# Scan layers of a four-layer network: the coefficients made inside the recurrence's phase, and another end for the last block

## What is computed

```python
xr, gate = split(x @ W_in.T, 2)                     # 1024 columns each
xc = silu(causal_conv4(xr + t_emb) + b_conv)
xn = layernorm(xc) * ln_g + ln_b
Bm, Cm, dt = split(xn @ W_xproj.T, 3)               # 16 states each
dt = tanh(dt @ W_dt.T + b_dt) * 0.01
Ad = 1.0 - dt * tanh(A_log)
Bd = Bm * minimum(norm(xn), 1.0)
h = clip(h * ad[:, :, None] + bd[:, :, None] * xt[:, None, :], -10.0, 10.0)   # 128 steps
yt = einsum('bd,bdh->bh', ct, h)
out = (ys + D * xn) * silu(gate) @ W_out.T
```

## Time and profile before

| | us |
|---|---|
| median of 3 runs | 4326.25 (4320.41, 4326.63, 4326.25) |
| the profiled execution | 4321.35, span 4319.3 |
| TensorE, matmuls, busy | 3880.4 (90%) |
| VectorE busy | 2926.8 (68%) |
| GpSimd busy | 1807.9 (42%) |
| ScalarE busy | 1318.1 (31%) |
| DMA, mean | 144 GB/s, 620 MB |
| granted TensorE clock, mean | 0.938 |

### The profile page before, as it was taken

The page is one execution under the profiler, slowest core; times in us unless marked ns, Lnnn a source line. Parts: engine busy times, 40 slices in busy tenths (PEclk is TensorE's granted clock), DMA queues, the critical chain, the costliest instruction groups (busy, mean ns, idle before and its releaser), DMA issues. The chain is left out here.

```text
span 4319.3 us, 67813 instructions
## 1 busy us (share of the span) xinstructions
PE 3880.4 (90%) x24096; PEld 2388.2 (55%) x24096; DVE 2926.8 (68%) x3026; ACT 1318.1 (31%) x1957; POOL 1807.9 (42%) x1456
## 2 busy tenths in 40 slices
PE   8999729999997899999889999997999819999999
PEld 6776403334333677777666777765777503343334
DVE  4666458999995666666456656643666548999996
ACT  3554301111111433333243333323554401111111
POOL 2555425555554133332312333332455425555554
PEclk9999858999999899999979999998999958999999
DMA  3665545556553222221221222223566555655663
GB/s 114 227 227 218 214 148 181 183 186 193 176 182 122 80 63 78 75 74 62 76 97 57 75 74 74 67 69 124 189 228 229 209 170 171 193 175 183 188 192 105
DMA packets 270819, 620.34 MB, mean 144 GB/s; under 512 B 34144, under 2 KB 37216, under 8 KB 270592
## 3 DMA queue, kind: packets, MB, share of 16 engines
q1 hardware_dynamic: 270592, 617.26, 43.1%
HBM read 380.71 MB, written 236.45 MB: 143 GB/s over the span
## 5 line engine op out<-in xcount | busy, mean ns | idle before, releaser
L1123 DVE CUSTOM_DVE_ANT_0 l0r_g<-l0r_g,l0r_pv,l0r_cf 128x1024 f32<-128x1024 f32 x512 | 674.3, 1339 | 76.5 <-PE l0r_pv L985 52.1
L1123 DVE CUSTOM_DVE_ANT_0 l3r_g<-l3r_g,l3r_pv,l3r_cf 128x1024 f32<-128x1024 f32 x512 | 674.1, 1339 | 75.5 <-PE l3r_pv L985 51.8
L985 PE MATMUL l0r_pv<-l0r_x,l0r_wv 32*128 32x512 f32 x1024 | 261.4, 510 | 26.3 <-POOL l0r_wv L910 20.8
L985 PE MATMUL l3r_pv<-l3r_x,l3r_wv 32*128 32x512 f32 x1024 | 260.6, 509 | 25.6 <-POOL l3r_wv L910 20.1
L997 PE MATMUL l0r_py<-l0r_g,l0r_cd 128*32 128x512 f32 x2048 | 282.0, 623 | 1.3 <-POOL l0r_cd L923 1.3
L997 PE MATMUL l3r_py<-l3r_g,l3r_cd 128*32 128x512 f32 x2048 | 281.1, 622 | 1.0 <-POOL l3r_cd L923 1.0
L985 PEld LDWEIGHTS l0r_pv<-l0r_x,l0r_wv 32*128 32x128 f32 x1024 | 97.2, 187 | 327.9 <-issue 224.8
L985 PEld LDWEIGHTS l3r_pv<-l3r_x,l3r_wv 32*128 32x128 f32 x1024 | 96.9, 186 | 326.3 <-issue 223.5
L1779 DVE RECIPROCAL l1h_rec<-l1h_ps_o 128x256 f32<-128x256 f32 x64 | 112.3, 1754 | 121.8 <-PE l1h_ps_o L1480 121.7
L1779 DVE RECIPROCAL l2h_rec<-l2h_ps_o 128x256 f32<-128x256 f32 x64 | 112.3, 1754 | 120.4 <-PE l2h_ps_o L1480 120.4
L1858 POOL TENSOR_TENSOR l2h_st<-l2h_veps,l2h_mhalf 128x1 f32<-128x1 f32 x32 | 17.6, 548 | 391.7 <-DVE l2h_veps L1745 391.7
(11 more groups left out here) (427 smaller groups left out, 9871.2 us busy)
## 6 DMA issues: line engine op xcount, KB each, us to landing
xhl_s<-l0a_xo SPq DMA_DIRECT2D x128, 512.0 KB, 4.6
l0r_x<-xhl_s SPq DMA_DIRECT2D x128, 512.0 KB, 11.7
xhl_s<-l3a_xo SPq DMA_DIRECT2D x128, 512.0 KB, 4.6
l3r_x<-xhl_s SPq DMA_DIRECT2D x128, 512.0 KB, 11.7
gate_s<-l0a_gate SPq DMA_DIRECT2D x64, 256.0 KB, 3.4
dx_s<-l0a_dx SPq DMA_DIRECT2D x32, 512.0 KB, 5.1
l0r_crow<-feed_s SPq DMA_DIRECT2D x64, 256.0 KB
l0r_dx<-dx_s SPq DMA_DIRECT2D x32, 512.0 KB, 13.3
```

The lines of the kernel that those rows point to most:

```text
L985: last = pe.matmul(pv[j % 2][:, h * HALF:(h + 1) * HALF], wv[r, q, 2 * t + j % 2, :], x[r, q, t, j % 2, :], start=True, stop=True)
L1123: dve._custom_dve(bass.dve_ops.TENSOR_ADD_SAT, out=g[:, t, j, :], in0=g[:, (t - 1) % TS, j, :], in1=pv[j % 2][:, :], s0=cf[:, q, t, 0, j:j ...
```

## The change

The coefficient phase goes; its body stands at the start of each engine's program in the recurrence's phase. Its large tiles become parts of `g`, `zh`, `zl` and `pv`, which the recurrence doesn't need yet. SP loads the constants, then x of blocks 0 and 1, dx and gate of block 0, and only then waits for `feed`, stores it and loads `crow` of both blocks. VectorE's chain has three of its steps in another place: the copies before the norm; the readers' factor before the bounds; the negative bound behind the feed's low half. GpSimd waits for `const` and the chain's 19th step before `bounds(0)`.

At the end TensorE turns block 30's second half, does the four half read-outs of block 31, then block 30's mix with block 31's first turn after its fourth slot, the second turn, and block 31's mix. VectorE, which has nothing to do after the last clamp-add, adds dx and multiplies by gate straight from `py`, in two halves of 512 columns; ScalarE makes `zh` straight from `pz` (without `zt`), VectorE `zl` from `pz` too, and VectorE adds the mix's result in `po` to the residual's rows. `keep_y(31)`, `gating(31)`, both `low(31, ..)`, `keep_out(31)` and `residual(31)` go. SP loads block 31's rows before it stores block 30.

```diff
         coef = keep.sb("coef", [P, S, 3, GJ])
-        coefficient_phase(nc, tag + "b", w, cst, dram, proj, stat, wsum, wbias, coef)
-        recurrence_phase(nc, tag + "r", x_in, x_out, w, cst, dram, coef)
+        recurrence_phase(nc, tag + "r", x_in, x_out, w, cst, dram, proj, stat, wsum, wbias, coef)
...
+        mean_w = g[:, 0, 0:2, :].rearrange("p a d -> p (a d)")[:, 0:B * NPROJ].rearrange("p (b c) -> p b c", b=B)
+        parts = [g[:, 0, 2, 0:512], g[:, 0, 2, 512:1024], g[:, 0, 3, 0:512]]
+        decay, prod, inv, feed = (g[:, 1, c // 2, c % 2 * 512:c % 2 * 512 + 512].rearrange("p (j s) -> p j s", j=GJ) for c in range(4))
+        zero = g[:, 1, 2, 0:S]
+        feed_h, feed_l = (z[:, 0:GJ, :] for z in (zh, zl))
+        pt = (pv[0][:, 0:512], pv[0][:, 512:1024], pv[1][:, 0:512])
+        pf = pv[1][:, 512:1024]
+        alog_ld, root, step, turned, tanh = (ph.sem(n) for n in ("alog_ld", "root", "step", "turned", "tanh"))
...
+            sp.dma_start(ident[:, :], cst["ident"]).then_inc(const, 16)
+            for b in range(GB):
+                sp.dma_start(alog[b * NS:(b + 1) * NS, :], w["A_log"].rearrange("(n a) -> n a", a=1)).then_inc(alog_ld, 16)
             sp.dma_start(same[:, :], cst["same"]).then_inc(const, 16)
             sp.dma_start(ymask[:, :, :], cst["ymask"]).then_inc(const, 16)
-            sp.dma_start(ident[:, :], cst["ident"]).then_inc(const, 16)
+
+            def store_feed():
+                feed_w = dram["feed"].rearrange("a c s (p i) -> s c a p i", p=2)
+                sp.wait_ge(feed_high, 1)
+                sp.dma_start(feed_w[:, 0, :, :, :], feed_h.bitcast(F32).rearrange("s (a p) i -> s a p i", a=2)).then_inc(stored, 16)
+                sp.wait_ge(feed_low, 1)
+                sp.dma_start(feed_w[:, 1, :, :, :], feed_l.bitcast(F32).rearrange("s (a p) i -> s a p i", a=2)).then_inc(stored, 16)
+                sp.wait_ge(stored, 32)
...
                     if first and q == 0:
+                        load_x(0, 0)
+                        load_x(1, 1)
+                        load_tokens(0, 0)
+                        store_feed()
                         load_feed(0, 0)
-                        load_x(0, 0)
-                    if not (last and q == 1):
-                        load_feed(k + 1, 1 - q)
-                        load_x(k + 1, 1 - q)
-                    load_tokens(k, q)
+                        load_feed(1, 1)
+                    else:
+                        if not (last and q == 1):
+                            load_feed(k + 1, 1 - q)
+                            load_x(k + 1, 1 - q)
+                        load_tokens(k, q)
...
+            load_rows(NBLK - 1, 1, n_pairs - 1)
             store(NBLK - 2, 0)
-            load_rows(NBLK - 1, 1, n_pairs - 1)
-            store(NBLK - 1, 1)
+            sp.wait_ge(last_res, 1)
+            sp.dma_start(x_out[(NBLK - 1) * P:NBLK * P, :], xr[:, 1, :]).then_inc(o_st[1], 16)
...
+            pool.wait_ge(step, 8 + 3 + GJ + 1 + 3)
...
             low(NBLK - 2, 1)
-            gating(NBLK - 1, 1, n_pairs)
             residual(NBLK - 2, 0, n_pairs)
-            low(NBLK - 1, 0)
-            low(NBLK - 1, 1)
-            residual(NBLK - 1, 1, n_pairs)
...
+            def turn_last(part):
+                pe.wait_ge(last_z, part + 1)
+                if part == 0:
+                    pe.wait_ge(z_ev, 2 * NBLK - 2)
+                else:
+                    pe.wait_ge(z_lo, 2 * NBLK - 1)
...
             blocks(pe, n_pairs, body)
-            for t in range(TS):
-                for j in range(GJ):
-                    if j % 2 == 0:
-                        between(NBLK, t, j, False, 0)
-                    elif t < LAG:
-                        read_out(NBLK - 1, t - LAG + TS, 1, j // 2)
-            turn(NBLK - 1, 1)
+            turn(NBLK - 2, 1)
+            for t in range(TS - LAG, TS):
+                for h in range(2):
+                    read_out(NBLK - 1, t, 1, h)
+            for slot in range(len(MIX)):
+                mix(NBLK - 2, slot)
+                if slot == 3:
+                    turn_last(0)
+            turn_last(1)
...
-            keep_y(NBLK - 1)
             keep_out(NBLK - 2)
-            high(NBLK - 1, 0)
-            high(NBLK - 1, 1)
-            keep_out(NBLK - 1)
+            for part in range(2):
+                act.wait_ge(z_mm, 2 * NBLK - 1 + part)
+                act.wait_ge(o_mm, NBLK - 1)
+                act.activation(zh[:, part * GJ:(part + 1) * GJ, :].rearrange("p k s -> p (k s)"), pz[:, :], ACT.Copy).then_inc(z_hi, 1)
...
+            chain(dve.tensor_copy(part[2], proj[:, :, 2 * NS:NPROJ]))
+            chain(dve.tensor_copy(part[1], proj[:, :, NS:2 * NS]))
+            dve.wait_ge(root, 2)
+            chain(dve.tensor_scalar(norm[:, :], norm[:, :], 1.0, None, ALU.min))
+            chain(dve.tensor_tensor(part[0], proj[:, :, 0:NS], norm[:, :].unsqueeze(2).to_broadcast([P, B, NS]), ALU.mult))
...
+            dve.wait_ge(turned, 1)
+            dve.tensor_tensor(feed, turn[0], inv, ALU.mult).then_inc(fed, 1)
+            chain(dve.tensor_tensor(out[2], turn[1], prod, ALU.mult))
+            chain(dve.tensor_scalar(out[0], inv, CLIP, None, ALU.mult))
+            dve.wait_ge(feed_high, 1)
+            dve.tensor_tensor(feed_l.rearrange("s j i -> s (j i)"), pf, feed_h.bitcast(F32).rearrange("s j i -> s (j i)"),
+                              ALU.subtract).then_inc(feed_low, 1)
+            chain(dve.tensor_scalar(out[1], inv, -CLIP, None, ALU.mult))
             dve.memset(g[:, TS - 1, :, :], 0.0).then_inc(gup, GJ)
...
+            dve.wait_ge(ymm, TS * NBLK)
+            dve.wait_ge(dx_ld[1], 16 * n_pairs)
+            dve.wait_ge(g_ld[1], 16 * n_pairs)
+            dve.wait_ge(z_mm, 2 * NBLK - 2)
+            for h in range(2):
+                c = slice(h * HALF, (h + 1) * HALF)
+                dve.tensor_tensor(y[:, c], py[:, c], dx[:, 1, c], ALU.add).then_inc(last_sum, 1)
+                dve.wait_ge(last_sum, h + 1)
+                dve.tensor_tensor(y[:, c], y[:, c], gate[:, 1, c], ALU.mult).then_inc(last_z, 1)
+            for part in range(2):
+                c = slice(part * GJ, (part + 1) * GJ)
+                dve.wait_ge(z_hi, 2 * NBLK - 1 + part)
+                dve.tensor_tensor(zl[:, c, :].rearrange("p k s -> p (k s)"), pz[:, :],
+                                  zh[:, c, :].bitcast(F32).rearrange("p k s -> p (k s)"), ALU.subtract).then_inc(z_lo, 1)
+            dve.wait_ge(o_mm, NBLK)
+            dve.wait_ge(xr_ld[1], 16 * n_pairs)
+            dve.tensor_tensor(xr[:, 1, :], xr[:, 1, :], po[:, :], ALU.add).then_inc(last_res, 1)
```

More of the change, by code:

```diff
@@ L978, in _ @@
             pe.wait_ge(const, 48)
+            pe.wait_ge(step, 8)
+            for c in range(3):
+                for j in range(GJ):
+                    last = pe.transpose(pt[c][:, j * S:(j + 1) * S], parts[c][:, j * P:(j + 1) * P], ident[:, :])
+            last.then_inc(turned, 1)
+            pe.wait_ge(fed, 1)
+            for j in range(GJ):
+                last = pe.transpose(pf[:, j * P:(j + 1) * P], feed[:, j, :], ident[:, :])
+            last.then_inc(feed_turned, 1)
             def spread(s, t, q, j):
@@ L1005, in turn @@
                 at_least(pe, z_ev, 2 * k + part)
+                for c in range(GJ):
+                    last = pe.transpose(pz[:, c * P:(c + 1) * P], y[:, (part * GJ + c) * P:(part * GJ + c + 1) * P], ident[:, :])
+                last.then_inc(z_mm, 1)
+            def turn_last(part):
[4 more added lines that the diff above has]
+                    pe.wait_ge(z_lo, 2 * NBLK - 1)
                 for c in range(GJ):
@@ new lines, in _ @@
+            chain(dve.tensor_tensor(proj[:, :, :], proj[:, :, :], wbias[:, :].unsqueeze(1).to_broadcast(full), ALU.add))
+            part = [c.rearrange("p (b n) -> p b n", b=B) for c in parts]
+            chain(dve.tensor_copy(part[2], proj[:, :, 2 * NS:NPROJ]))
[3 more added lines that the diff above has]
+            chain(dve.tensor_tensor(part[0], proj[:, :, 0:NS], norm[:, :].unsqueeze(2).to_broadcast([P, B, NS]), ALU.mult))
@@ new lines, in _ @@
+            chain(dve.memset(zero, 0.0))
+            dve.wait_ge(tanh, 2)
+            chain(dve.tensor_scalar(acol[:, 1:2], acol[:, 0:1], -0.01, None, ALU.mult))
+            chain(dve.tensor_scalar(decay, decay, acol[:, 1:2], 1.0, ALU.mult, ALU.add))
+            for j in range(GJ):
+                chain(dve.tensor_tensor_scan(prod[:, j, :], decay[:, j, :], zero, 1.0, ALU.mult, ALU.add))
+            chain(dve.reciprocal(inv, prod))
+            out = [coef[:, :, c, :].rearrange("p s j -> p j s") for c in range(3)]
@@ new lines, in _ @@
+            turn = [pt[c].rearrange("p (j s) -> p j s", j=GJ) for c in range(2)]
+            dve.wait_ge(turned, 1)
[5 more added lines that the diff above has]
+                              ALU.subtract).then_inc(feed_low, 1)
```

123 lines of the change are left out of this document (27 added, 96 removed).

## The result

| | before | after |
|---|---|---|
| first measurement, median | 4325.68 (4 runs) | 4283.77 (4277.03 to 4291.79, 4 runs) |
| ratio, 95% interval | | 0.9906 (0.9887 to 0.9925) |
| measured again, median | 4324.17 (11 runs) | 4286.54 (4278.46 to 4293.81, 6 runs) |
| ratio, 95% interval | | 0.9915 (0.9900 to 0.9930) |
| profiled execution, span | 4321.35, 4319.3 | 4283.66, 4281.9 |

A forecast was written before the change was run, and what follows sets the result against it. Bound: 512 VectorE clamp-adds of 1.34 us per scan layer, left alone, so only the loop's ends gain. (6+7.5+7)x2 = 41 us off the profiled 4321.35 gives 4280, plus 3 for the median: 4283; own range 4274 to 4292, overall 4268 to 4302.

The forecast's parts named there:

- Start: Head of each scan layer, coefficients to first weigh: weigh begins 6 us earlier per layer (1.5 to 8).
- crow itself: Block 0's broadcast rows in the head: 8.4 us from issue to weigh instead of 11.7 (bounds 7 and 11.7).
- The prefetch costs nothing: Head: ten early loads end at 599.1, before the store's issue at 600.9, hidden by 15 us of VectorE chain.
- rival A: Head: the queue isn't empty at the store, which lands 8 us late; gain 25 us, 4299; chance 0.11.
- Blocks 0 and 1: First two blocks of each scan layer: earlier W_outT and no stalls gain 7.5 us per layer (2 to 10).
- both stalls: TensorE's waits for GpSimd in block 1, 1.30 and 5.83 us: neither left, 2 us to spare on the second.
- The 32nd clamp-add: Sign in the first blocks: clamp-add 32 near offset 47 from the loop's start, where it ended by 55.
- Rival B: Blocks 0 and 1: W_outT still slow or second stall back; gain 28.6 us, 4296; chance 0.15.
- Tail: Last block, last clamp-add to the end: reordered read-outs and VectorE's finish gain 7 us per layer.
- the lower branch: Tail, if TensorE's clock still falls in the last mix: 3.1 us back, a gain of 5.3.
- the 22 to 25 that were to show it: Sign in the tail: 22 to 25 us from the last clamp-add to the span's end, where it was 30.8.
- Rival D: Blocks 1 to 3: TensorE's clock falls and stays at half, making the kernel slower, 4324 and more; chance 0.03.

The follow-up runs named there:

- e2: The kernel before with the new tail alone: 4313.41 us, ratio to before 0.9967.
- e5: The kernel before with only TensorE's order of the last block's work changed, read-outs ahead of block 30's mix: 4310.54 us.
- e1: The changed kernel with the old tail, so the new head alone: 4302.23 us, ratio to before 0.994.
- e7: The changed kernel with the last block's z in tiles of its own, so ScalarE makes zh before copying block 30's result: 4285.55 us.
- e11: The changed kernel itself, measured and profiled once more: 4286.54 us.
- e4: The changed kernel with only block 1's x load moved behind the feed's stores and both blocks' crow: 4288.26 us.
- e10: e9 plus 32 unread products before the first spread, and unread products for missing mixes, turns and read-outs in blocks 0 and 1: 4277.57 us.
- e12: e10 with three unread products instead of four in the mix slots and in place of read-outs: 4266.88 us, ratio to before 0.9863.
- e9: The changed kernel with e6 and e7 together, and ScalarE's queue issuing the second half of block 0's crow: 4273.01 us.
- e6: The changed kernel with each 64-row broadcast load of crow cut into four of 16 rows: 4285.74 us.

## Why the prediction was right

Point by point, after the steps of the prediction.

- **Start: 6 taken, 5.5 and 4.4 measured** in the two layers. Over all profiles with the old head (before, e2, e5: six starts, mean 38.3) and the new one (after, e1, e7, e11: eight, mean 33.75) it is 4.6. The low half ended at 601.44 (forecast 601.65), crow was issued at 603.65 (604.0). The mis-sized term is crow itself: 9.3 us from issue to weigh for 8.4, inside its bounds of 7 to 11.7. I had summed it at the rate of the 2.4 us where crow was alone, but its pair for block 1 and W_outT share the queue. That this is the reason wasn't tried; between 604.8 and 610.4 the slices show 56 to 133 GB/s for all of them.
- **The prefetch costs nothing: right**, though for other numbers. SP needed 5.6 us for the ten issues, not 15.1; most likely what had held it between the earlier trace rows was the queue, full of crow and x. The data were there at about 599.4 (599.1). The stores were issued 1.3 us later, and rival A (a queue that isn't empty) didn't come about. The Trainium skill (DMA: Bandwidth & Descriptors, Specifications) gives a limit of about 358 GB/s per core, by which it would have been 600.6, an estimate; the slices show up to 425, and the measurement decides.
- **Blocks 0 and 1: 7.5 taken, 6.5 and 7.4 measured.** SP left W_outT at offset 17.5 (19), the last low weight was done at 21.9 (24), both stalls were gone, as forecast. The 32nd clamp-add ended at 48.9 in layer 0, where TensorE's clock stayed at half to offset 51, and at 47.2 in layer 3, for 47; in e11's layer 0, with the rise at 32, it ended at 45.4. Rival B didn't come about, but e4 shows how near it was. Over the profiles above the term is larger: third store at 124.8 (six) against 115.7 (eight), 9.1 us. The profile of before that I worked from was a good one for its kernel. Not all of this is the stalls: the clock is at half for 55 us on the mean in the six and for 44 in the eight, and among the twelve starts with the early loads 10 us more at half go with a third store some 4 us later. By that, an estimate, some 4 of the 9.1 us come with the clock. Where the time at half is alike, 50 to 53 us, the third store is at 123.1 and 123.5 with the old head and at 116.6 and 118.4 with the new, 5 to 7 us earlier. The 7.5 us that I put down to the stalls and the clamp-adds are right as a mean, with that share of the clock in them.
- **Tail: 7 taken, 8.6 and 8.9 measured.** The two branches were right and I took the middle between them: 5.3 at half clock, 8.4 at full. It was full in both layers. Over the 14 tails that have the whole new order it is 21.7 to 22.0 in ten and 0.9 to 1.6 us longer in four, with the clock at half for 3.4 us; even so the gain is about 7, so the lower branch was priced too low. By the means it is 8.1 (30.4 in the four tails of before and e1, 22.2 in the 14). At 21.7 and 22.0 us from the last clamp-add to the end it is just below the 22 to 25 that were to show it. By its steps, from the last clamp-add's end: read-outs done 3.5 us (3.8), second half ready 6.3 (6.7), mix of block 30 done 9.6 (10.0), idle 1.99 (2.1), second turn done 12.2 (12.7), store 18.4 (19.2). What I hadn't seen is which edit does it: e5 shows that the order alone, and the clock with it, brings three quarters.
- **Rival D, the clock**, was the right place and a wrong sign. The clock does fall again in block 1, as the rival had it, when at full rate VectorE sets the pace: before the fall in e11's layer 3 TensorE is busy for 5.26 of 6.90 us. But it isn't a cost of the change, the old head has it too: stretches at half rate go on until 55 to 70 us after the loop's start with the old head and until 32 to 62 with the new. It is part of what makes the runs of one kernel differ by ±8 us, and no term of the sum had it.
- **Layer 1's attention** lost 3.8 us in the compared pair. Over all profiles it is 763.6 to 768.4 with the old head (three, mean 765.5) and 764.2 to 772.5 with the new (eleven, mean 767.9). A cost of 2 us that the change has there can't be excluded; nothing in the code leads to one.

41 us forecast, some 40 measured: by the means, the start was put too high by 1.4 us per layer, the middle and the tail too low by 1.6 and 1.1, and layer 1 gave 2.4 back. The sum was better than its terms; that part is luck.

## What to carry to other kernels

Price a merged phase by the queue, not by the barrier: what a load is behind, and what is behind it two waits further on, was worth more than the barrier. When a pipeline drains, put the work that others wait for first, and only then look for faster engines to finish it. And before a difference of a few microseconds is explained, profile the same program twice: here one stage moved by 5.5 us from one execution to the next and by 7.3 between two layers of one execution (e11), more than most edits to it.

## What the runs showed of the hardware

- **One program, many clocks.** The same instruction stream at the loop's start met the first rise of TensorE's clock at offset 15 to 51 us, in 19 of 22 starts a fall back to 1.2 GHz for 3 to 41 us, and the last rise at 32 to 70. In the changed kernel's layer 0 TensorE was busy for 30.81 of 30.90 us (635.33 to 666.23) at 1.2 GHz before the rise; at full rate it waits for VectorE between the parts. What follows the rise differs at nearly the same load: 5.26 of 6.90 us busy in e11's layer 3, then the fall; 5.48 of 7.00 us in its layer 0, and the full rate stayed. With unread full products in the gaps and ahead of the loop the clock rose 8 us before the loop in four of four starts, and was at full rate for good from offset 9 at the latest. The Trainium skill (TensorE: Matmul & The Clock Gate, Part 1) says that activity releases the throttle, and that the moment of the rise varies between runs, by half a microsecond in its example. e10 and e12 agree with the first; for the second the traces show tens of microseconds.
- **An idle time of 2 us can cost the clock.** After the tail's 1.99 us the clock stayed in ten of 14 cases and was at half for 3.4 us in four, which cost 0.9 to 1.6 us. After the 2 us ahead of the loop in e10 and e12 it stayed in two starts of four. Without the idle time (e7, e9, e10, e12: eight tails of 20.2 to 20.5 us) the tail kept its length each time.
- **A broadcast from 4 rows of DRAM is slow in its shape**: 0.52 MB in two transfers are used 9.3 us after the issue, and after 5.6 us as eight transfers of 16 rows (e6). A second queue brought nothing more (e9, 5.5 us).
